# First attention with plain maxima, channel-major outputs and a rebuilt output stage

## The reference

```
x = x + LN(attention1(LN(x)))      # 16 heads of 16 channels, rotary positions, full softmax
x = x + LN(ffn(LN(x)))             # two layers: windowed attention (8 heads of 64) and a gated MLP
```

```python
q, k, v = rope(proj(Wq, bq)), rope(proj(Wk, bk)), proj(Wv, bv)      # per head [2048, 16]
scores = einsum('bhtd,bhsd->bhts', q, k) / sqrt(16)
attn = softmax(scores); out = einsum('bhts,bhsd->bhtd', attn, v)
return einsum('btc,oc->bto', out, Wo) + bo
```

## Time and profile before

| | us |
|---|---|
| timed, median of 3 (lowest, highest) | 3234.95 (3229.55, 3236.52) |
| profiled execution, span from first to last instruction | 3219.8 |
| lies around the span, against the median | 15.15 |
| projection | 0 to 180 |
| first attention | 180 to 1627 |
| output stage | 1627 to 1709 |
| feed-forward and final sum | 1709 to 3220 |

### The profile page before, as it was taken

How to read it: one execution, slowest core, us unless ns; L and a number is a source line. 1 busy time by engine, 2 the same in 40 slices (tenths; PEclk the granted TensorE clock), 3 DMA queues, 4 the chain that set the end, 5 groups by cost and what they waited for, 6 DMA issues and landing times. The chain is left out here.

```text
span 3219.8 us, 63296 instructions
## 1 busy us (share of the span) xinstructions
PE 3012.8 (94%) x23672; PEld 1873.1 (58%) x23672; DVE 2490.0 (77%) x4820; ACT 2268.6 (70%) x4998; POOL 780.4 (24%) x1019
## 2 busy tenths in 40 slices
PE   8969999999999999999985999999999999999995
PEld 5733333333333333333354788888888888888884
DVE  4668899999989999899445767677777767777774
ACT  3407788888878888788875767676667767676663
POOL 4510000000000000000054434343434434343432
PEclk9958999999989999999997999999999999999998
DMA  3333212333322233322040000000000000000002
GB/s 115 112 82 41 38 25 41 41 41 41 41 32 32 40 41 41 41 41 41 12 161 23 1 1 0 0 0 0 0 1 35 1 1 0 0 0 0 0 1 71
DMA packets 47115, 99.37 MB, mean 31 GB/s; under 512 B 17184, under 2 KB 29472, under 8 KB 40480
## 3 DMA queue, kind: packets, MB, share of 16 engines
q1 hardware_dynamic: 42400, 95.48, 15.6%
q10 hardware_dynamic: 4544, 1.38, 0.2%
HBM read 71.13 MB, written 25.69 MB: 30 GB/s over the span
## 5 line engine op out<-in xcount | busy, mean ns | idle before, releaser
L691 DVE TENSOR_REDUCE mx<-aux 128x1 f32<-128x1024 f32 x1024 | 1246.5, 1224 | 116.4 <-PE aux L556 108.8
L661 ACT ACTIVATE probs<-scores 128x512 f32<-128x512 f32 x2048 | 1118.5, 597 | 250.1 <-PE scores L580 143.2
L556 PE MATMUL aux<-k_stack,q_stack 48*128 48x512 f32 x2048 | 792.8, 466 | 27.7 <-DMA k_stack<-qk_dram 19.5
L580 PE MATMUL scores<-q_stack,k_stack 50*128 50x512 f32 x2048 | 777.8, 456 | 13.4 <-ACT probs L661 13.4
L592 PE MATMUL pv<-probs,v_ones 128*32 128x256 f32 x8192 | 670.2, 400 | 0.1
L580 PEld LDWEIGHTS scores<-q_stack,k_stack 50*128 50x128 f32 x2048 | 317.3, 189 | 439.5 <-ACT probs L661 414.7
L592 PEld LDWEIGHTS pv<-probs,v_ones 128*32 128x32 f32 x8192 | 162.8, 109 | 373.6 <-ACT probs L661 275.8
L556 PEld LDWEIGHTS aux<-k_stack,q_stack 48*128 48x128 f32 x2048 | 320.5, 194 | 77.7 <-DVE mx L691 51.7
L522 POOL CAST m_parts<-head_max 128x16 fp32r<-128x16 f32 x32 | 6.3, 198 | 1355.9 <-DVE head_max L696 1355.9
L1241 PE MATMUL bank<-QO,w_sb 128*128 128x128 f32 x2816 | 328.2, 277 | 1.5 <-ACT QO L1328 1.5
L1241 PEld LDWEIGHTS bank<-QO,w_sb 128*128 128x128 f32 x2816 | 322.5, 193 | 2.5 <-ACT QO L1328 2.5
(11 more groups left out here) (175 smaller groups left out, 4628.2 us busy)
## 6 DMA issues: line engine op xcount, KB each, us to landing
q_stack<-qk_dram SPq DMA_DIRECT2D x192, 128.0 KB, 5.2
k_stack<-qk_dram SPq DMA_DIRECT2D x192, 128.0 KB, 6.8
qk_dram<-qkT_hi SPq DMA_DIRECT2D x32, 256.0 KB, 3.1
qk_dram<-qkT_lo SPq DMA_DIRECT2D x32, 256.0 KB, 3.6
out<-x_sb SPq DMA_DIRECT2D x9, 384.0 KB, 4.0
wqkv_sb<-in_wqkv SPq DMA_DIRECT2D x2, 1536.0 KB, 7.7
w_sb<-in_w SPq DMA_DIRECT2D x2, 1408.0 KB, 11.7
x_sb<-in_x SPq DMA_DIRECT2D x1, 2048.0 KB, 18.9
```

Of the source, the lines that this page charges most:

```text
L556: last = nc.tensor.matmul(aux[:, ring["unit"], block_of_keys % 2], q_stack[rows, r % BODY, tile * P:(tile + 1) * P], k_stack[rows, r % BOD ...
L580: nc.tensor.matmul(scores[:, item % BANKS1], k_stack[0:SCORE_ROWS, r % BODY, s * P:(s + 1) * P], q_stack[0:SCORE_ROWS, r % BODY, j * 512:( ...
L661: nc.scalar.activation(probs[:, item % PROBS], scores[:, item % BANKS1], ACT.Exp, scale=float(D1) ** -0.5).then_inc(probs_ready, 1)
L691: nc.vector.reduce_max(mx[:, slot, tile, half:half + 1], aux[:, unit].rearrange("p a k -> p (a k)"), AX.X).then_inc(max_taken, 1)
```

## The change

- Projection: the rounded bias and its rest stand in rows 0 and 32 of one tile; one product of 128 rows with a matrix that picks these rows takes the place of two one-row products.
- Opening: 24 tiles of maxima ahead instead of 20.75. For them TensorE scores keys 0 to 1023 as before and forms, for each 512 of them, the difference to keys 1024 to 2047 with two accumulated products (the second with the negated q, made by GpSimd). ScalarE takes the positive part (Relu), VectorE adds it to the scores and takes the maximum in one instruction on 1024 columns.
- Heads: maxima as before (plain). All engines' streams are written out, without loop and without lowering of semaphores. The maximum rows are copied by VectorE and go to q straight from SBUF, in two DMAs. The output item is gone: 8 DMAs a head move `o_stage` to a channel-major tile `VO` and the sums, each repeated over 16 rows, to `totals`. For every eight heads VectorE inverts `totals` in four pieces of [128, 512], and GpSimd multiplies.
- Output stage: works on pairs of tiles, takes `VO` as the stationary operand with no gathering and no transposes, has the residual sum on GpSimd, and stores x1 once it is made.

```diff
-        bias_hi, bias_lo = sb("bqkv1_hi", [P, 3 * C], F32R), sb("bqkv1_lo", [P, 3 * C], F32R)
-        ones_row = sb("ones_row", [P, P], F32R)
+        bias_parts = sb("bqkv1_parts", [P, 3 * C], F32R)
+        picked = sb("picked_rows", [P, P], F32R)
...
-                    nc.vector.tensor_tensor(bias_lo[:], bias_sb[:], bias_hi[:], ALU.subtract).then_inc(w_split, 1)
+                    rows = slice(LOW_ROW, LOW_ROW + 32)
+                    nc.vector.tensor_tensor(bias_parts[rows], bias_sb[rows], bias_parts[rows], ALU.subtract).then_inc(w_split, 1)
...
-                        for n, part in enumerate((bias_hi, bias_lo)):
-                            nc.tensor.matmul(out, ones_row[0:1, :], part[0:1, columns], start=(n == 0), stop=False)
+                        nc.tensor.matmul(out, picked[:], bias_parts[:, columns], start=True, stop=False)
...
+SPAN = TB // 2
+SLOTS = SPAN * BLOCKS
+SPANS = NH * TB // SPAN
+AHEAD = 3
+OPENING = AHEAD * SPAN
+FIRST_ROWS = TB + 3
+ROWS_SLOT = 13
...
+            def move_outputs(n):
+
+                c, place = n // CHUNK, n % CHUNK * D1
+                sp.wait_ge(pv_copied, n + 1)
+                if n % CHUNK == 0 and c > 0:
+                    sp.wait_ge(divided, BLOCKS * c)
+                for j in range(BLOCKS):
+                    for to, row in ((outputs[place:place + D1, c], VW * j), (totals[place:place + D1], VW * j + D1)):
+                        sp.dma_start(to[:, j * 512:(j + 1) * 512], o_stage[row:row + D1, n % 2]).then_inc(outputs_moved, 16)
...
+            for n in range(NH):
+                sp.wait_ge(head_begun, n + 1)
+                if n + 1 < NH:
+                    load(n + 1, 0, for_scores_loaded)
+                if n + 2 < NH:
+                    load(n + 2, SECOND, for_max_loaded)
+                if n >= 1:
+                    move_outputs(n - 1)
+                if n + 1 < NH:
+                    load_rows(n + 1)
...
+            for n, start, stop in Q_MINUS_PIECES:
+                pool.wait_ge(for_max_loaded[n], 16 * LOADS)
+                nc.gpsimd.tensor_scalar(q_minus_first[max_rows, n * TB + start:n * TB + stop], q_stack[max_rows, n, start * P:stop * P].rearrange("p (t c) -> p t c", c=P).bitcast(F32),
+                                        -1.0, None, ALU.mult).then_inc(q_minus_made, 1)
...
+            def divide(c):
+
+                for j in range(BLOCKS):
+                    columns = slice(j * 512, (j + 1) * 512)
+                    pool.wait_ge(inverted, BLOCKS * c + j + 1)
+                    nc.gpsimd.tensor_tensor(out=outputs[:, c, columns], in0=outputs[:, c, columns], in1=totals[:, columns], op=ALU.mult).then_inc(divided, 1)
+                pool.wait_ge(divided, BLOCKS * (c + 1))
+
+            for n in range(NH):
+                maxima_and_values(n)
+                if n % CHUNK == 1 and n > 1:
...
+            def difference(t, k, out):
+
+                n, tile = divmod(t, TB)
+                piece = [i for i, (head, start, stop) in enumerate(Q_MINUS_PIECES) if head == n and start <= tile < stop][0]
+                pe.wait_ge(q_minus_made, piece + 1)
+                minus = q_minus_first[max_rows, t]
+                pe.wait_ge(for_max_loaded[n % BODY], 16 * LOADS * (n // BODY + 1))
+                nc.tensor.matmul(out, q_stack[max_rows, n % BODY, tile * P:(tile + 1) * P], k_stack[max_rows, n % BODY, (2 + k) * 512:(3 + k) * 512], start=True, stop=False)
...
+            for t in range(OPENING):
+                if t == FIRST_ROWS:
+                    maximum_rows(0)
+                for k in range(2):
+                    difference(t, k, for_act(2 * t + k))
+                for keys in range(2):
+                    for_dve(t, keys)
+
+            for p in range(SPANS):
+                for i in range(SLOTS):
+                    step, j = p * SPAN + i // BLOCKS, i % BLOCKS
+                    score(p * SLOTS + i)
+                    if i == 5 and p % 2 == 0:
+                        nc.tensor.nop().then_inc(head_begun, 1)
+                    if p < WITH_MAXIMA:
+                        for_dve((p + AHEAD) * SPAN + block_at[i][0], block_at[i][1])
+                    if rows_here(p, i):
+                        maximum_rows(p // 2 + 1)
                     if j == 0:
-                        weigh_earlier(r, d, s, 2, 1, left, first)
-                    if j == (3 if s == 1 else 2):
...
+            def positive_part(t, k, item):
+
+                act.wait_ge(act_filled, item + 1)
+                if t >= 2:
+                    act.wait_ge(dve_emptied, unit_of[t - 2, 0] + 1)
+                nc.scalar.activation(excess[:, t % 2, k], scores[:, item % BANKS1], ACT.Relu).then_inc(act_emptied, 1)
...
+            def take_joined_maximum(t, item):
+
+                n, tile = divmod(t, TB)
+                unit, above = unit_of[t, 0], excess[:, t % 2].rearrange("p a k -> p (a k)")
+                dve.wait_ge(dve_filled, unit + 1)
+                dve.wait_ge(act_emptied, item + 1)
+                nc.vector.tensor_tensor_reduce(out=above, in0=aux[:, unit % 2].rearrange("p a k -> p (a k)"), in1=above, scale=1.0, scalar=LOWEST,
+                                               op0=ALU.add, op1=ALU.max, accum_out=mx[:, n % BODY, tile, 0:1]).then_inc(dve_emptied, 1)
...
+            def copy_rows(n):
+
+                dve.wait_ge(dve_filled, rows_unit[n] + 1)
+                nc.vector.tensor_copy(m_rows[:], aux[0:2 * TB, rows_unit[n] % 2, 0, 0:P]).then_inc(rows_copied, 1)
+                dve.wait_ge(rows_copied, n + 1)
+                nc.vector.nop().then_inc(dve_emptied, 1)
+
+            def invert_totals(c, j):
+
+                dve.wait_ge(outputs_moved, 16 * 2 * BLOCKS * CHUNK * (c + 1))
+                here = totals[:, j * 512:(j + 1) * 512]
+                nc.vector.reciprocal(here, here).then_inc(inverted, 1)
...
+                    if p < WITH_MAXIMA and block_at[i][1] % 2 == 1:
+                        take_maximum((p + AHEAD) * SPAN + block_at[i][0], block_at[i][1] // 2)
+                    if p % 2 == 1 and i == 3 and n + 1 < NH:
+                        larger_half(n + 1)
+                    if rows_here(p, i):
+                        copy_rows(n + 1)
+                    if p % 2 == 1 and i % SPAN == SPAN - 1 and n % CHUNK == 0 and n > 0:
+                        invert_totals(n // CHUNK - 1, i // SPAN)
+            for j in range(BLOCKS):
+                invert_totals(NH // CHUNK - 1, j)
...
+            for t in steps:
+                if exists(t):
+                    inverse_deviation(0, t)
+                if exists(t - 2):
+                    inverse_deviation(1, t - 2)
+                if exists(t - 1):
+                    v = t - 1
+                    pool.wait_ge(y_normed_made, 2 * v + 2)
+                    nc.gpsimd.tensor_tensor(out=x1_sb[:, pair(v)], in0=y_normed[:, v % 2], in1=x_sb[:, pair(v)], op=ALU.add).then_inc(x1_made, 1)
...
+                        last = nc.tensor.matmul(psY[:, v % 4, i], outputs[:, b * NC + k, t * P:(t + 1) * P], w_sb[:, k], start=False, stop=(k == NC - 1))
+                last.then_inc(y_done, 1)
```

More of the change, by code:

```diff
@@ new lines, in for_act, with for_dve @@
+            def for_act(item):
+                if item >= BANKS1:
+                    pe.wait_ge(act_emptied, item - BANKS1 + 1)
+                return scores[:, item % BANKS1]
+            def for_dve(t, keys):
+                unit = unit_of[t, keys // 2]
+                if keys % 2 == 0 and unit >= 2:
+                    pe.wait_ge(dve_emptied, unit - 1)
+                last = score_for_max(t, keys, aux[:, unit % 2, keys % 2])
+                if keys % 2 == 1:
+                    last.then_inc(dve_filled, 1)
@@ L644, in _, with weigh_earlier @@
[L644 to L646 removed]
+            def weigh_earlier(step, back, half):
+                if step >= back and step - back < NH * TB:
+                    weigh((step - back) // TB, (step - back) % TB, half)
@@ L648, in _ @@
+            weigh_earlier(NH * TB, 2, 1)
+            weigh_earlier(NH * TB, 1, 0)
+            weigh_earlier(NH * TB + 1, 2, 1)
         @block.scalar
         def _(act):
[L651 to L661 removed]
@@ L709, in head @@
-            def head(r, n, left):
-                if r == 0:
-                    taken[0] = start
-                for at, (d, s, j, kind, what) in enumerate(aux_items(left)):
-                    unit = (first_unit(left) + at) % UNITS
-                    if kind == "max":
-                        take_max((r + what[0]) % BODY, what[1], what[2], unit)
-                    if kind == "out":
-                        write_output(r, n, unit)
-            units = [("max", u) for u in range((AHEAD + BLOCKS * LEAD) // 2)]
```

561 lines of the change are left out of this document (223 added, 338 removed).

## The result

The changed kernel takes 3451.38 us (median of 4; 3443.96 to 3474.07) against 3235.73 for the kernel before: ratio 1.071, 95% interval 1.066 to 1.077. I had forecast 3226, and 3168 to 3268 as the range. The profiled execution, 3474.07 us, is the slowest of the four. In the table further down the medians are of all runs, while the ratios leave out slow runs (more than 1.5% above the fastest of the same kernel), of which b1 and e5 have one each and e12 five of ten. First the page of the changed kernel: span, granted clock, and the groups that answer to the earlier trace rows (busy us, mean ns; idle before and who ended it).

What follows compares the result with a forecast made beforehand. VectorE and TensorE were taken to bind the heads together. Terms -34 + 9 - 66 + 70 + 19 - 5 = -7 us gave 3228 us, set to 3226 for likelier better ends; range 3168 to 3268.

Steps and rivals of the forecast that it cites:

- The opening runs 24 instead of 20.75 tiles ahead: Heads: the maxima's longer lead over the rest was priced at 0.5 us and ignored.
- Projection, -34: Projection: one bias product for two saves 1.09 us in 27 tiles, 1.5 in five slow ones; bounds -20 to -45.
- Opening, +9: Before the first exponential: 24 tiles, TensorE-bound at half clock, 63 us instead of 54.0; bounds +15 to -20.
- Heads, -66: Heads: output item gone -26 us, loop turns gone -15, clock falls with them -25.
- the turns' gaps: Heads: ten turns of the three-head loop, 1.5 us each, go with unrolling, -15 us.
- Reciprocals, +70: Heads: twelve wide reciprocals at 3.44 us, +41 us, plus lower clock behind three groups, +29 (bounds 0 and +60).
- End, +19: Behind the last head: copy, moves, four reciprocals and multiplication take 21.6 us instead of 2.4; bounds +8 and +25.
- Output stage, -5: Output stage: a pair of tiles takes 3.75 us instead of 4.05, 16 x 0.3; bounds -12 and +10.
- A: Rival on the reciprocals: they are cheap, 0.7 us each, giving about 3155 us; chance 0.10.
- D: Rival in the heads: unrolled ScalarE and VectorE code stalls as often, so -40 goes, 3266 us; chance 0.05.
- B: Rival: clock rises in opening (first half) or stays up behind reciprocals; one gives 3198 us, both 3170; chance 0.25.
- C: Rival in the heads: reciprocals with lasting low clock cost 36 us a group, not 23; 3259 to 3270; chance 0.25.

Runs made afterwards that it cites:

- b1: The kernel before with only the changed projection (one bias product of 128 rows in place of two one-row products): 3183.21 us, ratio 0.987.
- e5: The changed kernel with VectorE's maxima read over 448 of each 512 keys, the other keys left out: 3355.05 us, ratio 1.036.
- e12: Kernel with weighing behind the unit, gathered sums, plain opening and short end, plus one long TensorE wait a head before the rows' transpose: 3264.01 us, ratio 1.004.
- e1: The changed kernel with the weighing behind each maximum unit's second key block, not between its two; outputs' copy one slot later: 3191.15 us, ratio 0.988.
- e3: e1 with each of the 16 reciprocals cut from 512 columns to 16, part of the division left out: 3109.23 us, ratio 0.963.
- b2: The kernel before with its loop over three heads written out on every engine, semaphore lowering kept: 3214.81 us, ratio 0.996.
- e9: The changed kernel, weighing where it was, with the 16 reciprocals cut to 16 columns, the rest left out: 3411.66 us, ratio 1.059.
- e11: The changed kernel without the maxima's rows in the heads; later heads load the first head's rows: 3333.88 us, ratio 1.034.
- e2: The kernel before with the weighing put between each maximum unit's two key blocks, outputs' copy one slot later: 3592.28 us, ratio 1.112.

## Why the prediction was wrong

One step failed: "The opening runs 24 instead of 20.75 tiles ahead: 0.5 us, ignored." I read the 3.25 tiles as work brought forward, and not as a shift of the ring's units against the slots. It cost 260 us (e1). The order in a step stands in the code, and the earlier trace rows with 15 reads without a pause said that the old order just fitted, but nowhere did I ask which slots a unit's two blocks fall into. None of my four rivals had it.

The other steps can be read from e1 and e3, where that one is put right. e1's profiled span is 27 us under the one of before; I had -7 for the sum. The 15.15 us that I laid around the span did no harm, but they are mostly the difference between two executions: the profiled execution of the changed kernel took 3474.07 us with a span of 3472.3.

- **Projection, -34:** -50 in the trace, -48 in b1, beyond my bound. I assumed that the slow start lasts to 52 us and that the tile shortens by 1.09 us. The copies are 3.10 us apart and not 4.25 in the steady state, 27 x 1.15 = 31 us, where I had 27; the other 19 come from the first tiles (I had 7.5), since TensorE's full speed is there from the second tile on (its products 0.23 us apart from 20.3 us, copies at 20.32, 22.98, 25.66).
- **Opening, +9:** 63.7 us from the block's start to the first exponential became 75.1, +11.4. A tile took 2.56 us, at the half clock, as worked out. "GpSimd's new negation", 0.3 us, was wrong: TensorE's first product comes 10.4 us after the block's start (9.7 before), but VectorE's first maximum waits until 147.8 us for GpSimd, which fills the maxima's tile behind 8.4 us of negations. From there it is 57 us.
- **Heads, -66:** in e3 first to last exponential is 76 us shorter than before. The clock part was there (57 us at half speed, 24 us), and the turns' gaps went, but not because the loop did (b2); the lowering of the semaphores went too, which no run tested alone. A head without output item takes 40.53 us in e1 and 40.60 in e3, I had 40.7.
- **Reciprocals, +70:** 3.34 us each (I had 3.44); all of it cost 81 us in e1's heads and 7 behind them, between the profiles of e1 and e3. The clock fell behind each of the three groups, 48 to 68 us at half speed. The sum was 11 us too small, and its two parts were off against each other. I had 41 us for the reciprocals themselves, with only 1.9 us of slack for each of three in a group: the slack took all of those three, and only the first of a group lengthened its head, by 3.0 us (43.53 against 40.53), 9 us in all. For the low clock I had 29 us, from 19 units or 41 us at half speed a group; the 177 us that were measured in all cost 76. (The expectation of e3 gives my price as 3.34 us; it was 3.44.) The Trainium skill, "VectorE: DVE Perf Modes", "First, the fixed hardware budget", has a repeat count of 8, an estimated 4.3 us. At its 0.96 GHz the measured 3.34 us for 512 elements is 6.3 cycles an element, so the rows decide against taking the repeat count for eight cycles.
- **End, +19:** from the last exponential to the output stage's first product with Wo 11.6 us became 28.9, +17.
- **Output stage, -5:** from that product to the feed-forward's first 76.6 us became 66.2, -10.

Of the rivals, A and D fell (the reciprocals are dear; straight-line code has no stalls in e1). B's first half fell, the clock stayed low through the opening, and C's mechanism was seen in e1, but for less than its price (27 us a group, C had 36). The range of 3168 to 3268 would have held e1 and b1; it had no room for a step priced at nothing that wasn't.

## What to carry to other kernels

When a producer fills a ring of two buffers in pieces, look which other work falls *between the pieces* of one buffer and which *between two buffers*: only the second kind overlaps with the consumer. A lead, an offset or an unrolling that changes parity moves it from one to the other, and then costs on every item, here 0.19 us x 976 at the full clock. If TensorE and its consumer are both full, a wait is dear by the clock too: here one of 0.65 us with a fall of 20 us behind it cost 20 x 0.343 = 7 us more, and in e12 a single wait a head was enough for falls.

## What the runs showed of the hardware

- The granted clock fell to half behind 13 of 25 waits of 0.65 us (changed kernel) and 16 of 27 (e9), behind 20 of 30 waits of 1.44 to 1.62 us (e12), behind 6 of 24 of 0.53 us (e5), and behind none of some 445 waits in e11 in which the weight load alone stood 0.2 to 0.3 us. A fall lasted 3 us (kernel before) to 133 us (e2), and one of 20 us cost 7 to 9 us.
- A reciprocal of [128, 512] took 3.34 us on VectorE, in SBUF, where a maximum over 1024 columns from PSUM took 1.22 us.
- GpSimd's negation of 48 partitions took 1.5 us for 512 columns and 4.1 us for 1536.
- A product of 512 columns with one row of weights was dearer than one with 128 rows, and so was the first behind it: 0.32 and 0.34 us from start to start, where the others are 0.23 us apart. TensorE's timeline of the kernel before:

```profile
99.22 0.39 PE L301 MATMUL psQK<-bqkv_lo,ones_row 1*128 1x512 f32 x1
99.54 0.51 PE L304 MATMUL psQK<-wqkv_hi,xT_hi 128*128 128x512 f32 x1
99.88 0.40 PE L304 MATMUL psQK<-wqkv_lo,xT_hi 128*128 128x512 f32 x1
```

The first product of a tile is no proof of it. In the changed kernel it has 128 rows and takes 0.32 us too:

```profile
109.86 0.48 PE L307 MATMUL psQK<-bqkv_parts,picked_rows 128*128 128x512 f32 x1
110.18 0.40 PE L310 MATMUL psQK<-wqkv_hi,xT_hi 128*128 128x512 f32 x1
110.41 0.40 PE L310 MATMUL psQK<-wqkv_lo,xT_hi 128*128 128x512 f32 x1
```
